# The experts' second product in split fp32r parts for the 20 late groups, one group behind the first product

## What is computed

```
xs = layernorm(x).reshape(T, 256)                    # T = 1024 tokens
weights, sel = top_k(xs @ Wg, 2);  weights = softmax(weights)
h     = relu(einsum('td,edf->etf', xs, W1) + b1)     # 8 experts, hidden width 1024
out_e = einsum('etf,efd->etd', h, W2) + b2
out   = einsum('tk,tkd->td', weights, out_e[sel, token])
x     = x + out
```

## Time and profile before

| | us |
|---|---|
| median of 3 runs | 1333.5 |
| lowest and highest | 1330.9, 1334.74 |
| the profiled execution, its own time | 1332.68 |
| its span, first to last instruction | 1330.9 |
| mean granted TensorE clock | 0.992 |

### The profile page before, as it was taken

The page is one execution under the profiler, slowest core; times in us unless marked ns, Lnnn a source line. Parts: engine busy times, 40 slices in busy tenths (PEclk is TensorE's granted clock), DMA queues, the critical chain, the costliest instruction groups (busy, mean ns, idle before and its releaser), DMA issues.

```text
span 1330.9 us, 43417 instructions
## 1 busy us (share of the span) xinstructions
PE 1286.4 (97%) x18116; PEld 1139.2 (86%) x18116; DVE 892.7 (67%) x1866; ACT 581.6 (44%) x1234; POOL 591.0 (44%) x619
## 2 busy tenths in 40 slices
PE   6899999999999999999999999999998999899996
PEld 3489989899898898998989989889887787799996
DVE  5787777777777787787877778778665366521111
ACT  5244454444544544445444454454443233333332
POOL 2565455555455554555545556455432132222221
PEclk8999999999999999999999999999999999899999
DMA  6153433434343434434343434343453521476663
GB/s 217 36 122 74 121 88 96 118 73 117 79 107 89 105 83 113 105 89 107 79 117 74 116 80 107 90 105 81 115 133 66 210 77 61 144 218 183 190 169 82
DMA packets 71617, 147.61 MB, mean 111 GB/s; under 512 B 17320, under 2 KB 45680, under 8 KB 69232
## 3 DMA queue, kind: packets, MB, share of 16 engines
q1 hardware_dynamic: 67344, 139.71, 39.6%
q0 software_dynamic: 4080, 5.13, 2.5%
HBM read 62.79 MB, written 15.94 MB: 59 GB/s over the span
## 4 chain that ended last, share of the span: by engine, by line
PE 91%; DVE 3%; DMA 2%; POOL 1%; issue 1%; ACT 1%; SPq 0%; POOLq 0%; ACTq 0%; DVEq 0%
PE bank L1125 28%; PE bank L1153 9%; PE bank L1155 9%; PE bank L1113 9%; PE bank L1154 9%; PE bank L1397 6%; PE bank L1410 6%; PE bank L1165 4%; PE bank L1139 2%; PE bank L1132 2%; PE bank L1232 2%; PE bank L1183 2%; PE bank L1267 1%; DMA ksw<-kw 1%; PE bank L1309 1%
## 5 line engine op out<-in xcount | busy, mean ns | idle before, releaser
L440 POOL TENSOR_TENSOR kr<-kr,ksw 128x1024 f32<-128x1024 f32 x128 | 318.6, 2489 | 465.4 <-DVE pr L759 347.3
L1153 PE MATMUL bank<-x_hi,p_hi 128*128 128x258 f32 x1024 | 300.8, 294 | 0.0
L1155 PE MATMUL bank<-x_hi,p_lo 128*128 128x258 f32 x1024 | 288.5, 282 | 0.0
L1154 PE MATMUL bank<-x_lo,p_hi 128*128 128x256 f32 x1024 | 287.9, 281 | 0.0
L1125 PE MATMUL bank<-ct_hi,wk_hi 128*128 128x512 f32 x512 | 213.7, 417 | 0.4 <-DVE ct_lo L787 0.4
L1125 PE MATMUL bank<-ct_hi,wk_lo 128*128 128x512 f32 x512 | 201.3, 393 | 0.0
L1125 PE MATMUL bank<-ct_lo,wk_hi 128*128 128x512 f32 x512 | 200.6, 392 | 0.0
L775 DVE TENSOR_TENSOR kw<-bank,stab 128x1024 f32<-128x1024 f32 x128 | 156.7, 1224 | 61.9 <-PE bank L1125 61.9
L1154 PEld LDWEIGHTS bank<-x_lo,p_hi 128*128 128x128 f32 x1024 | 194.7, 190 | 0.0
L1155 PEld LDWEIGHTS bank<-x_hi,p_lo 128*128 128x128 f32 x1024 | 193.7, 189 | 0.0
L1153 PEld LDWEIGHTS bank<-x_hi,p_hi 128*128 128x128 f32 x1024 | 193.2, 189 | 0.0
(11 more groups left out here) (189 smaller groups left out, 1925.4 us busy)
## 6 DMA issues: line engine op xcount, KB each, us to landing
ksw<-kw SPq DMA_DIRECT2D x512, 128.0 KB
raw<-in_ctx_dram SPq DMA_DIRECT2D x16, 1024.0 KB, 5.9
w_two<-in_L_ffn_W_dram SPq DMA_DIRECT2D x16, 1024.0 KB
x_slots<-fill SPq DMA_DIRECT2D x128, 64.5 KB, 3.3
w_all<-in_L_ffn_W_dram SPq DMA_DIRECT2D x4, 2048.0 KB, 14.8
wo<-in_L_ffn_W_dram SPq DMA_DIRECT2D x7, 1024.0 KB
xs<-x_slots SPq DMA_DIRECT2D x23, 129.0 KB, 2.2
acc<-raw SPq DMA_DIRECT2D x9, 128.0 KB, 1.7
```

What stands on the lines that cost most here:

```text
L440: pool.tensor_tensor(kr[:, i], kr[:, i], ksw[:, i], ALU.add).then_inc(kr_done, 1)
L1153: pe.matmul(psZ[:, 0:D + 2], p_hi[:, i, c], x_hi[:, b, t], start=(t == 0), stop=False, skip_group_check=True)
L1154: pe.matmul(psZ[:, 0:D], p_hi[:, i, c], x_lo[:, b, t], start=False, stop=False, skip_group_check=True)
L1155: last = pe.matmul(psZ[:, 0:D + 2], p_lo[:, i, c], x_hi[:, b, t], start=False, stop=(t == ST - 1), skip_group_check=True)
```

## The change

For the late groups the second product is made in three fp32r products of parts. The parts of W2 of the group's expert and of h are made anew for each group. ACT copies the whole W2 of the expert to w2_hi. POOL makes slices 0 to 2 of w2_lo, behind add_rows of the group before, and DVE slices 3 to 7. DVE makes h_hi and h_lo in two halves (split). Each of these has two buffers. PE does hidden(g), then half of the second product of group g - 1, then the transposes for g + 1, then the other half. So everything behind the second product, weighting and adding, comes a group later than before. The new buffers lie where those of the middle stage lay (vbd, xn, qkT, wqkvT, feat_q, feat_k, am and others), and some semaphores are merged to make room for the new ones.

```diff
+            def second_low(g):                                   # gpsimd
+                e = expert_of(pool, g)
+                if g == EARLY:
+                    pool.wait_ge(w_ps, TT)
+                if g >= EARLY + 2:
+                    pool.wait_ge(e_ps, g - 1)
+                pool.wait_ge(w2_hi_done, g - EARLY + 1)
+                pool.tensor_tensor(w2_lo[g % 2][:, 0:3], w2_all[:, bass.ds(e, 1), 0:3].rearrange("p o f d -> p (o f) d"),
+                                   w2_hi[g % 2][:, 0:3].bitcast(F32), ALU.subtract).then_inc(w2_lo_pool, 1)
-            for g in range(1, GROUPS):
+            for g in range(1, EARLY - 1):
                 add_rows(g)
+            for g in range(EARLY, GROUPS):
+                add_rows(g - 1)
+                second_low(g)
+            add_rows(GROUPS - 1)
...
+            def second_high(g):                                  # scalar
+                e = expert_of(act, g)
+                ...
+                act.copy(w2_hi[g % 2][:], w2_all[:, bass.ds(e, 1)].rearrange("p o f d -> p (o f) d")).then_inc(w2_hi_done, 1)
...
                 hidden(g, 0, FT)
+                if g >= EARLY:
+                    second_high(g)
...
+            def split(g, c):                                     # vector
+                ...
+                dve.wait_ge(relu_done, FT * g + (c + 1) * FT // 2)
+                if g >= EARLY + 2:
+                    dve.wait_ge(e_ps, g - 1)
+                n = 2 * (g - EARLY) + c + 1
+                half = slice(c * FT // 2 * ROWS, (c + 1) * FT // 2 * ROWS)
+                h = raw[:, 1, g % 2 * 4 + 2 * c:g % 2 * 4 + 2 * c + 2].rearrange("p t d -> p (t d)")
+                dve.tensor_copy(h_hi[:, g % 2, half], h).then_inc(h_split, 1)
+                dve.wait_ge(h_split, 2 * n - 1)
+                dve.tensor_tensor(h_lo[g % 2][:, half], h, h_hi[:, g % 2, half].bitcast(F32), ALU.subtract).then_inc(h_split, 1)
+            def second_low(g):
+                ...
+                dve.tensor_tensor(w2_lo[g % 2][:, 3:FT], w2_all[:, bass.ds(e, 1), 3:FT].rearrange("p o f d -> p (o f) d"),
+                                  w2_hi[g % 2][:, 3:FT].bitcast(F32), ALU.subtract).then_inc(w2_lo_dve, 1)
+            rows_turned(EARLY + 1)
+            split(EARLY, 0)
+            split(EARLY, 1)
+            second_low(EARLY)
+            for g in range(EARLY + 1, GROUPS):
+                split(g, 0)
+                second_bias(g - 1)
+                numbers_of(g - 1)
+                split(g, 1)
                 if g + 1 < GROUPS:
                     rows_turned(g + 1)
-                weighted_rows(g)
+                weighted_rows(g - 1)
+                second_low(g)
...
+            def rows_out_parts(g, first, end):                   # tensor
+                if first == 0:
+                    pe.wait_ge(ys_done, g)
+                    pe.wait_ge(w2_lo_pool, g - EARLY + 1)
+                    pe.wait_ge(w2_lo_dve, g - EARLY + 1)
+                    pe.wait_ge(h_split, 4 * (g - EARLY + 1))
+                for f in range(first, end):
+                    rows = slice(f * ROWS, (f + 1) * ROWS)
+                    pe.matmul(bank[:, 4, 0:D], h_hi[:, g % 2, rows], w2_hi[g % 2][:, f], start=(f == 0), stop=False)
+                    pe.matmul(bank[:, 4, 0:D], h_hi[:, g % 2, rows], w2_lo[g % 2][:, f], start=False, stop=False)
+                    last = pe.matmul(bank[:, 4, 0:D], h_lo[g % 2][:, rows], w2_hi[g % 2][:, f], start=False, stop=(f == FT - 1))
+                if end == FT:
+                    last.then_inc(e_ps, 1)
+            hidden(EARLY, 0, FT)
+            rows_turned(EARLY + 1)
-            for g in range(EARLY, GROUPS):
+            for g in range(EARLY + 1, GROUPS):
                 hidden(g, 0, FT)
+                rows_out_parts(g - 1, 0, FT // 2)
                 if g + 1 < GROUPS:
                     rows_turned(g + 1)
-                rows_out(g)
+                rows_out_parts(g - 1, FT // 2, FT)
+            rows_out_parts(GROUPS - 1, 0, FT)
```

More of the change, by code:

```diff
@@ L83, in build @@
         feat_w = sb("feat_w", [P, 2, P])
-        vbd = sb("vbd", [P, 2, AH, 2 * (AD + 1)])
+        with ExitStack() as middle:
+            vbd = sb("vbd", [P, 2, AH, 2 * (AD + 1)], F32, middle)
+        h_lo_0 = sb("h_lo_0", [P, 2 * AH * 2 * (AD + 1)], F32R)
         o_part = sb("o_part", [P, N])
@@ L132, in build @@
         lin = ctx.enter_context(ExitStack())
[L133 to L136, removed]
+        with ExitStack() as middle:
+            xn = sb("xn", [P, 2, D], F32, middle)
+            xnT = sb("xnT", [P, 2, KC, P], F32, middle)
+            att = sb("att", [P, 2, 2, P], F32, middle)
+            attT = sb("attT", [P, 2, 2, P], F32, middle)
+        h_hi = sb("h_hi", [P, 2, FT * ROWS], F32R, lin)
         xfT = sb("xfT", [P, 2, D], F32, lin)
-        qkT = sb("qkT", [P, 2, 4, P], F32, lin)
+        with ExitStack() as middle:
+            qkT = sb("qkT", [P, 2, 4, P], F32, middle)
+        h_lo_1 = sb("h_lo_1", [P, FT * ROWS], F32R, lin)
         st6 = sb("st6", [P, 2, TT, 6], F32, lin)
@@ L148, in build @@
         xsT = sb("xsT", [P, 2, KC, ROWS], F32, lin)
-        wqkvT = sb("wqkvT", [P, KC, 3 * D], F32, lin)
-        woutT = sb("woutT", [P, 2, D], F32, lin)
-        feat_q = sb("feat_q", [P, 2, 4, 2, P], F32, lin)
-        wo = sb("wo", [P, PAIRS, D], F32, lin)
-        feat_k = sb("feat_k", [P, 2, 4, 2, P], F32, lin)
-        am = sb("am", [P, 2, 2, APAIRS, N], F32, lin)
+        with ExitStack() as middle:
+            wqkvT = sb("wqkvT", [P, KC, 3 * D], F32, middle)
+            woutT = sb("woutT", [P, 2, D], F32, middle)
+            feat_q = sb("feat_q", [P, 2, 4, 2, P], F32, middle)
+        w2_lo_0 = sb("w2_lo_0", [P, FT, D], F32R, lin)
+        w2_hi_0 = sb("w2_hi_0", [P, FT, D], F32R, lin)
+        wo = sb("wo", [P, PAIRS, D], F32, lin)
+        with ExitStack() as middle:
+            feat_k = sb("feat_k", [P, 2, 4, 2, P], F32, middle)
+            am = sb("am", [P, 2, 2, APAIRS, N], F32, middle)
+        w2_hi_1 = sb("w2_hi_1", [P, FT, D], F32R, lin)
+        w2_lo_1 = sb("w2_lo_1", [P, FT, D], F32R, lin)
         b1_now = sb("b1_now", [P, 2, FT], F32, lin)
@@ L186, in build @@
         w1 = [w1_two[:, 0], w1_two[:, 1], wo[:].rearrange("p (k a) d -> p k (a d)", k=KC)]
+        w2_hi, w2_lo, h_lo = (w2_hi_0, w2_hi_1), (w2_lo_0, w2_lo_1), (h_lo_0, h_lo_1)
         xs = sb("xs", [P, XB, D + 2], F32, lin)
@@ L247, in build @@
             sem(n) for n in ("z_ps", "rz_done", "zn_done", "zt_ps", "zts_done", "o_ps", "o_half", "o_done"))
+        w2_hi_done, w2_lo_pool, w2_lo_dve, h_split = (sem(n) for n in ("w2_hi_done", "w2_lo_pool", "w2_lo_dve", "h_split"))
         y_ps, y_done, out_st, bo_ld, x2_ld, xbo_done = (sem(n) for n in ("y_ps", "y_done", "out_st", "bo_ld", "x2_ld", "xbo_done"))
@@ L619, in _ @@
                 if j == STEPS - 10:
-                    act.wait_ge(vec2_ps, 1)
-                    act.copy(vecs2[:], psT[:, 0:E * FT + 4]).then_inc(vec2_done, 1)
+                    act.wait_ge(vec_ps, 2)
+                    act.copy(vecs2[:], psT[:, 0:E * FT + 4]).then_inc(vec_done, 1)
                 if j in (STEPS - 9, STEPS - 8):
@@ L627, in _ @@
                     turned(0)
-            act.wait_ge(vec2_done, 1)
+            act.wait_ge(vec_done, 2)
             def keys_queries(t):
@@ L683, in hidden @@
                     act.activation(hT(g, f), h_bank(g, f), ACT.Relu, bias=b1_now[:, g % 2, f:f + 1]).then_inc(relu_done, 1)
+            def second_high(g):
+                e = expert_of(act, g)
+                if g == EARLY:
+                    act.wait_ge(w_ps, TT)
+                if g >= EARLY + 2:
+                    act.wait_ge(e_ps, g - 1)
+                act.copy(w2_hi[g % 2][:], w2_all[:, bass.ds(e, 1)].rearrange("p o f d -> p (o f) d")).then_inc(w2_hi_done, 1)
             attention_turned(TT - 1)
@@ L999, in early_counts @@
             def early_counts():
-                dve.wait_ge(early_ps, 1)
+                dve.wait_ge(count_ps, 1)
                 group_experts(bank[:, 4, 0:E], group_full, ALU.is_ge, 0, EARLY, 0)
@@ L1066, in _ @@
             slots(TT - 1)
-            dve.wait_ge(total_ps, 1)
+            dve.wait_ge(count_ps, 2)
             group_experts(bank[:, 7, E:2 * E], group_steps, ALU.is_gt, EARLY, LATE, 16, n_exp[:, 5])
@@ L1074, in _ @@
             rows_turned(3)
-            for g in range(3, GROUPS):
-                second_bias(g)
-                numbers_of(g)
+            def split(g, c):
+                if g == EARLY and c == 0:
+                    dve.wait_ge(w_ps, TT)
+                dve.wait_ge(relu_done, FT * g + (c + 1) * FT // 2)
+                if g >= EARLY + 2:
+                    dve.wait_ge(e_ps, g - 1)
[6 more added lines that the diff above has]
+            def second_low(g):
+                e = expert_of(dve, g)
+                if g == EARLY:
+                    dve.wait_ge(w_ps, TT)
+                if g >= EARLY + 2:
```

(16 more changed lines are left out.)

6 lines of the change are left out of this document (3 added, 3 removed).

## The result

The changed kernel takes 1348.92 us in the median of 4 runs (1348.16 to 1350.84), against 1333.7. The ratio is 1.0119, with a 95% interval of 1.0101 to 1.0137: 15 us slower. The forecast was 1356, range 1342 to 1374. The profiled execution has a span of 1346.9 us, 16.0 more than before.

What follows compares the result with a forecast made beforehand. PE bounded the kernel before; POOL's difference would bound the changed rounds. Fill 13.0, 18 rounds of 8.24 (148.3) and last group 7.6 make 168.9 against 144.96 us: +24, so 1356, range 1342 to 1374.

Steps and rivals of the forecast that it cites:

- The ring through POOL: Late rounds: second product, weighting, POOL's issue, POOL's difference, next second product set the round, forecast at 8.24 us.
- PE's gain: Second product: 24 fp32r products take 2.85 us instead of 3.35, so PE gains 0.50 us a round.
- I take the order copy, POOL, difference: Late rounds: DVE's copy of h precedes POOL's difference, DVE's difference follows; round 8.24 us, 48 in 100.
- rival 2: Late rounds: POOL's difference starts before DVE's copy of h; round 7.74 to 7.8, +15 us, 1348; 20 in 100.
- e+2.52: Time in a late round, counted in us from e, the second product's end; here POOL's difference was to start.
- a register load ... I take 0.1: On POOL between indirect issue and difference: a register load costs 0.1 us, bounds 0.02 and 0.65.
- The exclusion: DVE and POOL: whichever starts first holds the shared pair for its whole instruction, and the other waits.
- the 2.15 us for ACT's copy: Stage start: PE, its three banks filled, waits for ACT, delayed by its W2 copy; about 2.2 us, once.
- rival 5: Late rounds: PE's clock falls because PE idles 1.5 us a round; over 1400 us if halved; 3 in 100.
- Nothing but PE sets the round: Late rounds: POOL ends in time, so PE alone sets 6.74 us a round; -4 us, 1329; 7 in 100.
- The indirect issue itself is held up: On POOL: DVE's 1.52 us difference delays the indirect issue; round 9.4, +46 us, 1379; 6 in 100.
- rival 4: On POOL: the indirect issue is held up by DVE's 1.52 us difference; round 9.4, 1379 us; 6 in 100.

Runs made afterwards that it cites:

- e1: The changed kernel with PE taking POOL's slices 0 to 2 last in the second product and waiting for POOL's part only there: 1350.5 us.
- e5: The changed kernel with slices 0 and 1 of w2_lo (512 columns) on POOL and 2 to 7 on DVE: 1341.6 us.
- e9: The kernel of e1 with POOL's part of W2 also moved ahead of its indirect issue: 1329.1 us.
- e3: The changed kernel with DVE making all of w2_lo (2048 columns) and POOL none: 1326.9 us.
- e2: The changed kernel with POOL's part of W2 made ahead of its indirect issue for the group before: 1327.7 us.
- e10: The kernel of e2 with the last group's second product in fp32, without parts: 1326.1 us.

## Why the prediction came out as it did

**The ring through POOL was right.** Second product, weighting, POOL's issue, POOL's difference, next second product is what sets the round: PE's wait ends 0.07 us behind POOL's difference, and both ways of opening the ring remove the wait.

**PE's gain was right.** From 1239.88 to 1242.94 are 3.06 us, less 0.21 for the transposes 2.85 for the 24 fp32r products, as forecast, and PE's own round is 6.67 against 6.74.

**The step that failed: "I take the order copy, POOL, difference", a round of 8.24 us.** Measured 7.69. It went as in rival 2, POOL before DVE's copy of h, whose 7.74 to 7.8 is nearly the round and whose 1348 is the time. The two starts lay hundredths apart, as rival 2 says: the sum had POOL's difference at e+2.52 and DVE's copy at e+2.45. Its term "a register load ... I take 0.1" was wrong, for nothing lies between the issue and POOL's work. The difference ends 1.85 us behind the end of the issue and takes 1.84 alone, so its work counts from e+2.42, and the copy came at e+2.48. The row (0.02 us behind an issue of 0.97) pointed that way. POOL's end at e+4.27 in place of e+4.44 is the missing 0.1 and the 0.08 by which POOL's own 1.84 is shorter than the 1.92 of the sum.

What reserves POOL's turn is not settled. The record of its difference starts at e+1.90, 1.03 us after the start of the issue and inside the issue's 1.55. In e1 DVE's copy of h came 0.12 or 0.13 us behind that recorded start in most rounds, before the issue had ended, and waited; in three rounds it came 0.17 to 0.51 ahead of it, and in two of these it waited too.

So the time was forecast in the right range with the wrong order, which is luck in part. The forecast's own range of 1350 to 1363 was missed, if by 1 us only, and 1348.9 lies in 1342 to 1374 because that was drawn to take in rival 2. One reading was wrong too: by the earlier trace rows DVE's copy takes 0.79 ns a column and its difference 1.19, which is 1.5 times and not twice the rate. The order does not hang on it.

**The exclusion was right in kind.** The plainest number is the 2.08 us of a 0.42 us copy. e5 and group 3 show the waiting in both directions: POOL behind DVE's difference, and DVE's difference (3.06 us in place of 1.49) behind POOL. The Trainium skill's page "SBUF — State Buffer", section "Who interferes with whom", calls it an exclusive lock, in which the order of issue decides who is blocked; e1 against e9 agrees, where one line's place in POOL's program made the round 8.01 or 6.67 us.

**Terms of the sum.** Start of hidden(3) to the end of group 3's product: 13.0 forecast, 13.4 measured (1175.70 to 1189.13). But the reason was another one: not the 2.15 us for ACT's copy, for PE had not run out of banks. It waited 0.77 us for xsT before hidden(4), and 1.84 for the parts of W2. There DVE's difference was recorded as 3.06 us because POOL held it. 18 rounds: 148.3 forecast, 138.5 measured. Last group: 7.6 forecast, 8.96 measured, since PE's clock fell after 4.4 us of idling. That is rival 5's mechanism in the one place where I had not looked for it; in the rounds the clock stayed at 1.00. In all 168.9 forecast, 160.9 measured. The rounds came 9.8 us short of the forecast, and the two ends give 1.8 of it back.

**The other rivals.** "Nothing but PE sets the round" would have given 1329, I said. With the ring opened it is 1327 (e3) and 1328 (e2), and the fill and the last group do eat much of PE's gain, as it said. "The indirect issue itself is held up" did not happen in the changed kernel, for a reason of 0.09 us (below). ACT cost nothing, as forecast: 1.91 us for its copy, and PE's records show no wait for it in the rounds.

## What to carry to other kernels

When a precision split moves work from the engine that sets the time to three others, what counts is not their share of busy time but where each new piece stands in its engine's program. Here POOL's piece stood behind a step that waits for PE's last result, and a gain of 0.57 us a round (7.24 to 6.67) became a loss of 0.45; the same piece one line earlier gives the gain. A piece that depends on nothing recent goes ahead of the step that does. DVE's differences of two SBUF inputs, its copies from SBUF to SBUF, and POOL's differences stood in each other's way here, and are to be planned as one engine. A busy time far above the instruction's own time is the sign, but not the cause: POOL's 2.37 us for 1.84 us of work is the end of its own issue, not DVE. And the last item of a pipeline has nothing to hide its preparation, so it may be best left in its old form (3.5 to 4.5 us here).

## What the runs showed of the hardware that I had not expected

- **An indirect issue on POOL waits for a DVE difference that is already running, and not for one that starts after it.** In the kernel after, the issue starts 0.09 us before DVE's difference and takes its usual 1.55 us; in all of e3 too, with a difference of 2.29 us beside it. In e1 DVE's difference starts 0.36 us first (1236.60 to 1238.08), the issue is recorded as 2.55 us, and it ends at 1239.51, 1.43 us behind the difference. The pairs of e2, e9 and e10 give 1.42 to 1.46, but for one of 1.54 or 1.55 in each at the start of the stage. Three more pairs of e1, from the timeline (start and duration of DVE's difference, then of the issue), give 1.43, 1.43 and 1.44:

```
1204.34 1.48   1204.70 2.55
1220.34 1.48   1220.81 2.44
1276.47 1.48   1277.34 2.05
```

  The Trainium skill's page "SBUF — State Buffer", section "Who interferes with whom", infers that a two-input tensor_tensor does not stall descriptor work on POOL. These rows say that it does hold up the whole issue when it comes first. The issue also takes its row numbers from SBUF (result_no), and no run separates that from the descriptor work, so the inference is not refuted for the latter. What waits is the start of the issue and not its rest: in e2 it is recorded from 1234.98, DVE's difference ends at 1235.73, and the issue ends 1.43 later, with DVE's copy of h (1235.65, 0.41 us) and its h_lo (1236.10, 0.69 us) at their own times beside it. In the changed kernel DVE's difference comes only 0.09 us too late in most rounds to hold up the issue, as rival 4 had it.
- **The record of POOL's next instruction starts inside that of an indirect issue, but its work does not.** It starts 1.03 us after the issue, with 0.52 left of the issue's record, and ends as if it had begun with the issue's end (1.85 us behind it, 1.84 alone).
- **The granted clock fell after 3.3 us (e3) and 4.4 us (the changed kernel) without matmuls**, to 0.60 and 0.57 in the four us behind. It stayed at 1.00 in rounds with about 0.8 us of idling each.
